# First attention: the value products of a group in one run instead of two sets

## The reference, cut to what matters

```python
xn = group_norm(x)                                   # [8, 128, 1024]
qkv = einsum('oc,bcl->bol', qkv_w, xn) + qkv_b       # 8 heads x (q, k, v) x 16 channels
w = einsum('bct,bcs->bts', q * scale, k * scale)     # scores, 1024 x 1024 per head
w = softmax(w.astype(float32), axis=-1)
a = einsum('bts,bcs->bct', w, v)                     # the value products
x = x + einsum('oc,bcl->bol', proj_w, a) + proj_b
x = x + conv_block(group_norm(x))                    # then a convolution block,
t = tokens(x)                                        # a causal attention with routed experts,
...                                                  # a scan attention with routed experts
```

## Time and profile before

| what | us |
| --- | --- |
| median of 3 runs | 4058.59 |
| lowest and highest | 4056.32, 4060.82 |
| the profiled execution's own time | 4049.84 |
| its span, first to last instruction | 4048.0 |
| mean granted TensorE clock in it | 0.886 |

### The profile page before, as it was taken

How to read it: one execution, slowest core, us unless ns; L and a number is a source line. 1 busy time by engine, 2 the same in 40 slices (tenths; PEclk the granted TensorE clock), 3 DMA queues, 4 the chain that set the end, 5 groups by cost and what they waited for, 6 DMA issues and landing times. The chain is left out here.

```text
span 4048.0 us, 131348 instructions
## 1 busy us (share of the span) xinstructions
PE 3351.7 (83%) x54119; PEld 2132.4 (53%) x54119; DVE 3089.8 (76%) x7658; ACT 1857.2 (46%) x4392; POOL 1093.1 (27%) x1947
## 2 busy tenths in 40 slices
PE   5999999996699514996679999999679999998529
PEld 1333333222367412664357788877267788876414
DVE  7888788865766642556868999998868999997477
ACT  1666666673334101334456655554356655554200
POOL 1001001000000374551055544333056543332000
PEclk7999999998799656996579999999589999999659
DMA  6023233300000211224000000000000000000128
GB/s 145 24 48 54 39 54 54 54 8 6 0 1 1 87 51 50 67 69 156 1 9 15 9 9 9 9 4 6 4 8 15 9 9 9 9 4 9 47 74 302
DMA packets 102446, 155.92 MB, mean 39 GB/s; under 512 B 17060, under 2 KB 63017, under 8 KB 101824
## 3 DMA queue, kind: packets, MB, share of 16 engines
q1 hardware_dynamic: 87616, 120.28, 11.6%
q0 software_dynamic: 13088, 23.06, 2.0%
q10 hardware_dynamic: 1152, 4.19, 0.3%
HBM read 103.21 MB, written 45.30 MB: 37 GB/s over the span
## 5 line engine op out<-in xcount | busy, mean ns | idle before, releaser
L2079 ACT ACTIVATE s_E<-s_Y,s_M 128x9 f32<-128x9 f32 (+38 forms) x2048 | 656.6, 392 | 626.7 <-DVE s_M L1992 624.3
L365 DVE TENSOR_REDUCE half_max<-shared 128x1 f32<-128x512 f32 x1024 | 644.9, 684 | 89.0 <-PE shared L286 86.5
L1893 PE MATMUL g_x<-s_ik,s_iqm 128*32 128x1 f32 (+63 forms) x16384 | 676.4, 280 | 27.1 <-DVE g_o L1975 11.6
L482 ACT ACTIVATE E<-sc 128x1024 f32<-128x1024 f32 x512 | 496.7, 1021 | 268.8 <-PE sc L300 268.7
L1987 DVE SCALAR_TENSOR_TENSOR s_Y<-s_Y,g_x 128x9 f32<-128x9 f32 (+38 forms) x2048 | 578.7, 283 | 46.8 <-PE g_x L1893 1.2
L1905 PE MATMUL g_p<-mats,s_E 128*128 128x128 f32 x3072 | 448.1, 283 | 38.6 <-ACT s_E L2079 34.2
L1893 PEld LDWEIGHTS g_x<-s_ik,s_iqm 128*32 128x32 f32 x16384 | 395.1, 116 | 153.8 <-issue 79.4
L1905 PEld LDWEIGHTS g_p<-mats,s_E 128*128 128x128 f32 x3072 | 338.9, 144 | 104.4 <-ACT s_E L2079 60.4
L286 PE MATMUL shared<-ks,qs 96*128 96x512 bf16 x1024 | 373.5, 403 | 18.4 <-DVE half_max L365 13.3
L1992 DVE TENSOR_REDUCE s_M<-s_Y 128x4 f32<-128x8 f32 (+56 forms) x512 | 351.2, 686 | 0.8 <-DVE s_Y L1987 0.4
L2003 DVE TENSOR_TENSOR resid<-g_p,s_W 128x512 f32<-128x512 f32 x384 | 263.7, 687 | 59.7 <-PE g_p L1905 56.6
(11 more groups left out here) (353 smaller groups left out, 5227.2 us busy)
## 6 DMA issues: line engine op xcount, KB each, us to landing
e_spread<-d_gate SPq DMA_DIRECT2D x64, 512.0 KB, 6.1
d_parts<-parts SPq DMA_DIRECT2D x8, 1536.0 KB, 5.9
qs<-d_parts SPq DMA_DIRECT2D x96, 128.0 KB, 7.3
ks<-d_parts SPq DMA_DIRECT2D x96, 128.0 KB, 12.4
me_xg<-d_xs SPq DMA_DIRECT2D x144, 65.0 KB, 1.8
mc_yb<-d_ys SPq DMA_DIRECT2D x8, 1024.0 KB, 8.0
resid<-in_x SPq DMA_DIRECT2D x8, 512.0 KB, 8.2
rden<-d_den POOLq DMA_DIRECT2D x16, 256.0 KB, 3.7
```

The costliest lines, as they stand in the source:

```text
L365: dve.tensor_reduce(half_max[n // SETS % 2][:, idx // 2, idx % 2:idx % 2 + 1], bank("bm", n)[:, :], AX_X, ALU.max).then_inc(max_done, 1)
L482: act.activation(E[:, G % 2, h, :], sc[n % 2][:, :], ACT.Exp, scale=0.25).then_inc(exp_done, 1)
L1893: mm = pe.matmul(x_ps[u % 3][32 * b:32 * (b + 1), rho % 2, 0:n + 1], iqm[n // WINDOW % 2][:, b, x0:x0 + D, :], s.ik[:, b, rho, 0:n + 1], s ...
L2079: act.activation(E[:, m % 2, rho, 0:m + 1], Y[:, D * (m % YR) + rho, 1:2 + m], ACT.Exp, bias=M[:, D - 1 + D * m + rho:D + D * m + rho]).th ...
```

## The change

In the groups that have value products, both sets of the group before are issued in the first half, one behind the other; the second half has none. Their number, operands and waits stay as they are, and so do the orders of the other engines.

```diff
                         if G in event and half == (G in late):
                             pe_misc(pe, event[G])
-                        if 0 < G <= GROUPS:
-                            pe_av(pe, G - 1, half)
+                        if 0 < G <= GROUPS and half == 0:
+                            pe_av(pe, G - 1, 0)
+                            pe_av(pe, G - 1, 1)
                         maxima(1)
```

## The result

The changed kernel takes 4092.9 us (median of 5 runs), the one before 4056.3: 36.6 us more. The ratio is 1.0086 with a 95% interval of 1.0063 to 1.0110, which is 34.9 us. (One of the five, at 4885.3 us and a granted clock of 0.627, was disturbed; it counts in the median of 4092.9 but not in the ratio, and the other four have a median of 4091.0.) The profiled execution took 4089.1 us, against 4049.8 before: 39.3 more. Of these the attention has 38.5: its last exponential ends at 962.6 us instead of 924.1.

What follows compares the result with a forecast made beforehand. TensorE bounds the old order; in the new one VectorE frees three banks too late. Terms +6.3, +27.7, +2.8, +1.6, -6 and +8 made +40 on 4058.6: 4099 us, range 4081 to 4115.

Steps and rivals of the forecast that it cites:

- Plain groups: Groups without an extra step: late banks lengthen each from 5.68 to 5.85 us, +0.17, in 37 groups 6.3 us.
- Groups with a step: Extra step between third and fourth maximum waits for a bank: +0.42 us each, 66 groups, 27.7 us.
- "T" group: Its step stands behind the seventh maximum, away from the run: +0.2 us taken, 14 groups, 2.8 us.
- row_max: VectorE work, 13 times 0.12 us, had room before and now lies on the chain: +1.6 us.
- The stalls: Waits for the denominators' DMA in group 2 of six images: longer groups come off them, -6 us.
- the sign that I had named: At L384, the wait for the denominators' DMA was to be shorter by about 1 us in each of six.
- The tail: From group 118, without maxima, ScalarE is late: period 4.23 becomes 5.03 us, +0.80 in ten groups, +8.
- The saving: TensorE's sixteen value products in one run cost 1.95 us instead of 2.18: 0.23 us less per group.
- the walk through a group: TensorE and VectorE followed bank by bank through one group without an extra step: a period of 5.85 us.
- The pause: VectorE was to pause about 0.5 us once per group, instead of 0.3 twice.
- TensorE stays the bound: Rival: banks come free early enough, 118 groups at 0.23 us give 27 us less, 4031; chance 6%.
- The clock: Rival: granted clock falls to the lower level in the new tail, 23 us more, 4122; chance 7%.

Runs made afterwards that it cites:

- tail_split: The changed kernel, but from group 118 on the two sets of value products stand in their own halves again; 4076.7 us, ratio 1.0060 to the kernel before.
- half_after: The changed kernel with VectorE reducing only the first 256 of each maximum's 512 columns; 4030.0 us, ratio 0.9950 to the kernel before.
- b4_after: The changed kernel with four banks instead of three for maxima and steps, the first key tile's scores left out; 4043.1 us, ratio 0.9976 to the kernel before.
- mid: The changed kernel with the fourth maximum moved between the two sets of value products; 4110.9 us, ratio 1.0127 to the kernel before.
- step_last: The changed kernel with a group's extra step behind the sixteen value products instead of ahead of them; 4098.2 us, ratio 1.0121 to the kernel before.
- kept_before: The kernel before with the second reciprocal of an image one group later, its num step in group 5, proj in 13; 4026.0 us, ratio 0.9923.
- half_before: The kernel before with VectorE reducing only the first 256 of each maximum's 512 columns; 4031.5 us, ratio 0.9953 to the kernel before.
- kept_after: The changed kernel with the same moves of reciprocal, num and proj as kept_before; 4069.1 us, ratio 1.0032 to the kernel before.

## Why the prediction was right, point by point

Predicted 4099, range 4081 to 4115; measured 4092.9. From the kernel before, +40 was said, and +36.6 (profiled: +39.3) came.

- *Plain groups* +0.17: measured 5.85 for 5.68. *Groups with a step* +0.42: 7.13 for 6.72 in "a" and "proj". A "T" group grows by 0.53 (6.45 for 5.92), but the group behind it by less than its own kind, so that "T" and the row_max that always stands ahead of it cost about 0.2 together, where 0.2 + 0.12 was said; no group shows either alone. With row_max the sum was 38.4 for groups 1 to 117. Measured, the groups outside the stalls' twelve grow by 692.9 - 662.4 = 30.5, and those twelve by 6 x (0.18 + 0.83) = 6.1 without their waits (5.85 and 8.40 for 5.67 and 7.57, as kernels show them in images without a wait): 36.6.
- *The stalls* -6: without waits the twelve take 6 x 13.24 = 79.4 before and 6 x 14.25 = 85.5 after; they took 102.6 and 101.0, so 23.2 of waiting became 15.5, -7.7. The number is near, but that is in part luck. The step said that the DMA ends when it ends and that groups 1 and 2, longer by 0.84, come off VectorE's wait. That wait fell only from 18.3 to 16.1, since the chain from the copy to the reciprocal took 18.1 us on average instead of 17.7, and the sign that I had named, 1 us less in each of six, didn't come. More came from two things that I hadn't seen and that the last section shows: VectorE may now be 1.40 us late before TensorE has to wait, where it was 0.83, and the clock. A second execution of the same groups (tail_split) has 11.2 us of waiting in place of 15.5, so even the sum says little.
- *The tail* +8: +7.1 up to the last group and +1.2 in it, 5.03 for 4.23. The start gave 1.3 that no term had; tail_split has the new order and the old start (110.2 us to group 1, against 110.3 and 111.6), so that is scatter.
- *The saving* of 0.23 per group is real. It stands in the walk through a group, which has the run at 1.86 us: a plain group gains it and loses 0.40 to the banks. Once banks come free in time it shows by itself (half_after, b4_after: 5.67 to 5.46, 0.21).
- *The pause*: I wrote about 0.5 us, and it is 0.92. By my own walk r3 ends at 3.48 + 1.2 + 0.68 = 5.36 and r4 comes at 5.85 + 0.43 = 6.28, which is 0.92; the figure in the list of signs was not taken from the walk.
- *The rivals*: "TensorE stays the bound" is what half_after and b4_after would be, and even they don't gain 27 us, since the tail and the stalls take it. The clock didn't fall where the rival had it fall, in the new tail: 912 to 960 us has 1.00. It does fall for some microseconds in both kernels, in the stalls; the 1.00 that I read for 250 to 440 us ends just short of such a place.

The rule of the Trainium skill (TensorEngine Tiling (Array Packing), Key Properties: a change of mode drains TensorE) names a cost of a change without its size, and the traces bear a cost out: half as many changes gave 0.21 us per plain group where the banks didn't bind, and in mid, where they do, twice as many cost 0.24. It didn't decide the change, because the loss at the banks, 0.40, is larger. The groups' lengths followed the ends of the reductions, and a profile in which TensorE is busy 98% of the time didn't show how near they were.

## What to carry to other kernels

Before work on one engine is put together in a run, set its length against what the consumer has queued: buffers times the consumer's start-to-start spacing (here 3 x 0.60 against 2.17 us). If they don't cover it, that is a warning and not yet a loss: in half_after they cover far less, VectorE pauses for 1.75 us, and no plain group pays. So follow one period by hand, from each buffer's release to its next use; the cost is in the catching up. Moving one producer step elsewhere need not help (mid, step_last). And where a stall is set by a DMA and not by the engines, it can absorb losses and gains: look for it first. Moving its waiter (kept_before, -0.8%) was worth more than the new order gave even where the banks didn't bind (half_after against half_before, within the noise).

## What the runs showed that I had not expected

**A stall costs more than its wait, and an engine's slack hides part of it.** The reciprocal's wait in image 2, with the first product of TensorE that waits behind it. The first two rows are from the kernel before, the last two from the changed one:

```profile
332.70 0.35 DVE L384 RECIPROCAL rcol<-den 128x32 f32<-128x32 f32 x1 [2.27 <-DMA den<-d_den]
333.66 0.39 PE L286 MATMUL shared<-ks,qs 96*128 96x512 bf16 x1 [1.44 <-DVE half_max L365]
...
344.23 0.35 DVE L385 RECIPROCAL rcol<-den 128x32 f32<-128x32 f32 x1 [3.62 <-DMA den<-d_den]
345.18 0.39 PE L286 MATMUL shared<-ks,qs 96*128 96x512 bf16 x1 [2.22 <-DVE half_max L366]
```

TensorE waits 0.83 us less than VectorE before (2.27 - 1.44) and 1.40 less after (3.62 - 2.22), in each image in which both wait. Over the six images VectorE's waits go from 18.3 to 16.1 us, but TensorE's long ones from 13.3 to 7.9. The second cost is the clock. In image 3 of the kernel before, by window (the column with 0.50 is the granted clock), and then TensorE's timeline:

```profile
440.00:446.60 6.60, 6.41 (x19) 1.67 (x20) 4.27 (x8) 2.05 (x2) 1.06 (x2) 0.50 0.13 42
...
440.19 0.61 PE L286 MATMUL shared<-ks,qs 96*128 96x512 bf16 x1 [2.69 <-DVE half_max L365]
440.59 1.06 PE L300 MATMUL sc<-qs,ks 98*128 98x512 bf16 x2
441.45 1.06 PE L286 MATMUL shared<-ks,qs 96*128 96x512 bf16 x2
...
446.77 0.60 PE L286 MATMUL shared<-ks,qs 96*128 96x512 bf16 x2
447.20 0.59 PE L300 MATMUL sc<-qs,ks 98*128 98x512 bf16 x2
```

TensorE stands still for 2.69 us, the granted clock goes to its lower level (1.2 GHz) for 6.8 us, and two bf16 products take 0.86 us (440.59 to 441.45) instead of 0.43 (446.77 to 447.20). In the kernel before this happens in images 1, 3, 5 and 6, 17.1 us in all, after waits of 1.76 to 3.58 us, and not in images 2 and 4, where TensorE waits 1.44 and 1.38. In the changed kernel it happens in images 2 and 3, 13.7 us. Before, groups 3 and 4 together grow by 0.4 us more than TensorE's wait where the clock stays up, and by 2.0 to 3.2 us more where it falls; so of the 23.2 us of stalls before, some 7.5 are the clock's, an estimate: 9.1 us over the waits in the four images less 4 x 0.4. kept_before has 3.4 us at the lower level in its groups and kept_after none.

**A bank that comes free late costs TensorE time even where the matmul's own row shows no wait.** TensorE at an "a" step in half_before, and the loading of the step's weights there and in the kernel before:

```profile
363.93 0.38 PE L286 MATMUL shared<-ks,qs 96*128 96x512 bf16 x1
363.96 0.38 PEld L257 LDWEIGHTS shared<-xnb,mats 128*128 128x128 f32 x2
364.15 1.02 PE L257 MATMUL shared<-xnb,mats 128*128 128x512 f32 x2
365.10 1.07 PE L314 MATMUL acc<-E,vx 128*32 128x512 f32 x8
...
372.34 0.30 PEld L257 LDWEIGHTS shared<-xnb,mats 128*128 128x128 f32 x2 [0.41 <-DVE half_max L365]
```

The step starts 0.22 after the maximum and lasts 0.95, where the earlier trace rows have 0.29 and 1.06 for the same instructions in the kernel before. With the halved reductions, and with the fourth bank too, such groups take 6.53 instead of 6.72, 0.19 less. I had read 6.72 as TensorE's own length. In the kernel before, the step's weights are loaded only when a reduction has given the bank free (372.34, the moment at which the product starts), in half_before 0.19 us ahead of the product (363.96 and 364.15), and the step's two instructions stand 0.53 apart instead of 0.43. Why that gap widens as well stays open. 66 such groups are 12 us, and outside the stalls the groups of half_before are 12.3 us shorter than those of the kernel before. But this is not all of the 20 us that half_before gained, nor does it all arrive: the stalls take 6.2 back, the start gives 5.0, where the reductions follow each other without a pause, and the attention ends 11.4 us earlier (912.7 against 924.1). The rest lies outside the attention or is scatter.
